# Routing lists of a four-layer gated network on one Trainium2 core: bf16 operands with the token tile innermost, and no GpSimd share

## The reference

```python
def _L3_ffn_ref(x, router_w, w1, w2):
    HID, FFN, E, K = (256, 1024, 8, 2)
    N = B * T
    x_flat = x.reshape(N, H)
    C = max(1, int(1.25 * N / E * K))
    probs = jax.nn.softmax(x_flat @ router_w.T, axis=-1)
    top_v, top_i = jax.lax.top_k(probs, K)
    top_v = top_v / jnp.sum(top_v, axis=-1, keepdims=True)
    for k in range(K):
        ...   # a token's position among those of its expert, kept if below C
        h = gelu(einsum('ech,ehf->ecf', expert_in, w1), approximate=False)
        y = einsum('ecf,efh->ech', h, w2)
        out = out + tok * (gate * keep)[:, None]
x = x + tanh(g_ffn[3]) * _L3_ffn_ref(_layernorm(x), ...)
```

## Time and profile before

| what | value |
|---|---|
| median of 3 runs | 1907.35 us (1907.02 to 1913.06) |
| the profiled execution, its own time | 1903.68 us |
| its span, first to last instruction | 1901.9 us |
| mean granted PE clock over the span | 0.913 of full |
| busy: PE, DVE, ACT, POOL | 82%, 65%, 49%, 16% of the span |
| last feed-forward's routing, logits to `f3_idx` | from 1584.65 to about 1619.5 us of the span |

### The profile page before, as it was taken

One profiled execution on the slowest core, in us unless ns is written; L12 is line 12 of the kernel. 1 busy time (PEld: TensorE's weight loads), 2 busy tenths in 40 slices (PEclk: granted clock), 3 DMA queues, 4 the chain that ended last, 5 costly groups with the idle time before them and its releaser, 6 DMA issues.

```text
span 1901.9 us, 30702 instructions
## 1 busy us (share of the span) xinstructions
PE 1558.9 (82%) x10686; PEld 1192.3 (63%) x10686; DVE 1241.1 (65%) x2782; ACT 937.2 (49%) x2055; POOL 300.9 (16%) x367
## 2 busy tenths in 40 slices
PE   4899873994788873588887999999969984799997
PEld 3666652873555542345554677788855543799997
DVE  6666648214899998766663444536359987577775
ACT  3455540323776742245554612223249971577775
POOL 2101101431121100111110000000012111243333
PEclk8899985996899987789998999999979995899999
DMA  8455244227564511635524100000167736422222
GB/s 165 61 75 84 41 147 169 42 34 148 106 104 93 89 54 47 78 47 73 73 35 172 76 1 1 0 1 1 45 78 98 114 71 256 161 39 40 43 39 28
DMA packets 86261, 144.10 MB, mean 76 GB/s; under 512 B 14031, under 2 KB 69767, under 8 KB 82937
## 3 DMA queue, kind: packets, MB, share of 16 engines
q1 hardware_dynamic: 66121, 102.76, 24.3%
q0 software_dynamic: 20016, 39.71, 13.6%
HBM read 75.50 MB, written 27.66 MB: 54 GB/s over the span
## 4 chain that ended last, share of the span: by engine, by line
PE 53%; DVE 25%; DMA 9%; issue 6%; ACT 5%; SPq 2%; POOL 0%; ACTq 0%; POOLq 0%; DVEq 0%
PE ps L1408 13%; PE ps L1512 7%; PE ps L1524 5%; DMA Qpack<-QP 5%; PE ps L1377 4%; DVE probs L2293 3%; PE ps L1048 2%; PE ps L1289 2%; PE ps L995 2%; SPq L525 2%; PE ps L904 2%; PE ps L986 2%; PE ps L1298 2%; DVE hpart L2274 2%; DVE nmax L2206 2%
## 5 line engine op out<-in xcount | busy, mean ns | idle before, releaser
L359 POOL DMA_DIRECT2D Kpack<-KP x192 | 101.1, 534 | 949.2 <-PE ps L1408 383.4
L1647 ACT ACTIVATE pT<-ps 128x512 f32<-128x512 f32 x256 | 151.8, 606 | 192.7 <-PE ps L989 98.9
L986 PE MATMUL ps<-Qpack,Kpack 99*128 99x256 bf16 (+1 forms) x768 | 166.1, 283 | 20.7 <-ACT pT L1652 8.0
L1512 PE MATMUL ps<-xgT,XNT 128*128 128x128 f32 x1248 | 146.9, 277 | 0.0
L1512 PEld LDWEIGHTS ps<-xgT,XNT 128*128 128x128 f32 x1248 | 144.0, 193 | 0.0
L955 PE MATMUL ps<-Kpack,Qpack 97*128 97x256 bf16 x512 | 103.4, 288 | 47.9 <-DMA Qpack<-QP 18.8
L2194 DVE CUSTOM_DVE_ANT_0 Vb<-ps,mask_bf 128x256 bf16<-128x256 f32 x256 | 94.9, 419 | 50.0 <-PE ps L955 49.9
L1652 ACT ACTIVATE pT<-ps,nmax 128x256 f32<-128x256 f32 x256 | 120.6, 532 | 11.9 <-DVE nmax L2206 11.4
L1408 PE MATMUL ps<-partB,h 128*128 128x512 f32 x512 | 121.1, 396 | 1.4 <-ACT xn L1904 1.4
L1408 PE MATMUL ps<-partA,h 128*128 128x512 f32 x512 | 120.4, 396 | 0.0
L2190 DVE TENSOR_REDUCE mx<-ps 128x2 f32<-128x512 f32 x128 | 84.6, 685 | 52.7 <-PE ps L955 51.9
(11 more groups left out here) (323 smaller groups left out, 3622.7 us busy)
## 6 DMA issues: line engine op xcount, KB each, us to landing
Kpack<-KP POOLq DMA_DIRECT2D x192, 128.0 KB, 5.2
Qpack<-QP SPq DMA_DIRECT2D x192, 128.0 KB, 6.9
w<-in_w SPq DMA_DIRECT2D x16, 1024.0 KB, 6.1
ctxT<-in_ctxT SPq DMA_DIRECT2D x32, 256.0 KB, 8.2
h_rows<-in_h SPq DMA_DIRECT2D x16, 512.0 KB, 7.8
h<-h_rows SPq DMA_DIRECT2D x2, 4096.0 KB, 22.1
wd<-in_wd SPq DMA_DIRECT2D x4, 1536.0 KB, 14.8
xn_rows<-xn SPq DMA_DIRECT2D x16, 256.0 KB, 2.5
```

Source lines behind the costliest of these rows:

```text
L359: eng.dma_start(Kpack[j][DH * k:DH * (k + 1)].rearrange("d (e f) t -> d e (f t)", f=HALF), KP[par][:, part]).then_inc(done, 16)
L986: mm = pe.matmul(A[h % ring][:, t], Kpack[par][0:rows, h, t * P:(t + 1) * P], Qpack[par][0:rows, h], start=True, stop=L != 0)
L1512: mm = pe.matmul(bank[:, f % 4 * P:(f % 4 + 1) * P], w1_tile[k % 2][:, c, f * P:(f + 1) * P], xgT3[k % 2][:, c], start=c == 0, stop=c == K ...
L1647: act.activation(pT[h % 8][:], A[h % 2][:], ACT.Exp).then_inc(s["exp_done"], 1)
```

## The change

`lists3` becomes `[P, PAIRS3, 6, TILES3, NT]` and `hot3` `[P, PAIRS3, P, NT]`: the token tile's number is the innermost dimension, 16 bf16 elements next to one another. `place3` and `tile3` become bf16. A table `cols3` of 128x16 bf16 (each column number sixteen times in a row) and `col_t3` (0 to 15 in bf16) are written by ACT after the softmax's exponential into the free half of `XNT`. All of DVE's operands of these operations are then bf16 with a last step of one element, the broadcast one being an outer dimension. GpSimd's two operations go to DVE, and `f3_place` and `f3_gates` go away. PE's two operands of the 32 matmuls now have 16 elements (32 bytes) from one column to the next.

```diff
-        place3 = sb("place3", [P, PAIRS3, NT], F32, f3c)
-        tile3 = sb("tile3", [P, PAIRS3, NT], F32, f3c)
+        place3 = sb("place3", [P, PAIRS3, NT], BF16, f3c)
+        tile3 = sb("tile3", [P, PAIRS3, NT], BF16, f3c)
...
-        hot3 = sb("hot3", [P, PAIRS3, NT, P], BF16, l3c)
-        lists3 = sb("lists3", [P, PAIRS3, NT, 6, TILES3], BF16, l3c)
+        hot3 = sb("hot3", [P, PAIRS3, P, NT], BF16, l3c)
+        lists3 = sb("lists3", [P, PAIRS3, 6, TILES3, NT], BF16, l3c)
...
+        cols3 = XNT[:, 1, 0:P * NT // 2].bitcast(BF16).rearrange("p (c t) -> p c t", t=NT)
+        col_t3 = XNT[:, 1, P * NT // 2:(P + 1) * NT // 2].bitcast(BF16)
...
             def ffn3(n):                       # gpsimd
-                wide = [P, PAIRS3, NT, TILES3]
-                pool.wait_ge(s["f3_place"], 1)
-                for v in range(1, 3):
-                    e = pool.tensor_tensor(lists3[:, :, :, 3 + v], lists3[:, :, :, 0], part3[v][:].unsqueeze(3).to_broadcast(wide), ALU.mult)
-                e.then_inc(s["f3_gates"], 1)
                 rows_sent(n)
...
-                pe.wait_ge(s["f3_gates"], 1)
                 for j in range(PAIRS3):
                     pe.wait_ge(s["hot"], listed + j + 1)
                     for t in range(NT):
-                        mm = pe.matmul(ps[3][:].rearrange("p a b -> p (a b)")[:, 0:6 * TILES3], hot3[:, j, t],
-                                       lists3[:, j, t].rearrange("p v i -> p (v i)"),
+                        mm = pe.matmul(ps[3][:].rearrange("p a b -> p (a b)")[:, 0:6 * TILES3], hot3[:, j, :, t],
+                                       lists3[:, j, :, :, t].rearrange("p v i -> p (v i)"),
...
                 route_exp(3)                   # scalar
+                act.activation(cols3, col[:].unsqueeze(2).to_broadcast([P, P, NT]), ACT.Copy)
+                act.activation(col_t3, col[:, 0:NT], ACT.Copy).then_inc(s["f3_cols"], 1)
...
-                per = lists3[:, :, :, 0]       # vector
-                wide = [P, PAIRS3, NT, TILES3]
-                chain(dve.tensor_tensor(per, tile3[:].unsqueeze(3).to_broadcast(wide),
-                                        col[:, 0:TILES3].unsqueeze(1).unsqueeze(1).to_broadcast(wide), ALU.is_equal))
-                dve.sem_inc(s["f3_place"], 1)
-                dve.tensor_tensor(lists3[:, :, :, 1], per, col[:, 0:NT].unsqueeze(1).unsqueeze(3).to_broadcast(wide), ALU.mult)
-                dve.tensor_scalar(lists3[:, :, :, 2], per, row[:], None, ALU.mult)
-                dve.tensor_tensor(lists3[:, :, :, 3], per, part3[0][:].unsqueeze(3).to_broadcast(wide), ALU.mult)
+                per = lists3[:, :, 0]
+                wide = [P, PAIRS3, TILES3, NT]
+                dve.wait_ge(s["f3_cols"], 1)
+                chain(dve.tensor_tensor(per, tile3[:].unsqueeze(2).to_broadcast(wide),
+                                        cols3[:, 0:TILES3].unsqueeze(1).to_broadcast(wide), ALU.is_equal))
+                dve.tensor_tensor(lists3[:, :, 1], per, col_t3.unsqueeze(1).unsqueeze(1).to_broadcast(wide), ALU.mult)
+                dve.tensor_scalar(lists3[:, :, 2], per, row[:], None, ALU.mult)
+                for v in range(3):
+                    dve.tensor_tensor(lists3[:, :, 3 + v], per, part3[v][:].unsqueeze(2).to_broadcast(wide), ALU.mult)
                 for j in range(PAIRS3):
-                    dve.tensor_tensor(hot3[:, j], place3[:, j].unsqueeze(2).to_broadcast([P, NT, P]),
-                                      col[:].unsqueeze(1).to_broadcast([P, NT, P]), ALU.is_equal).then_inc(s["hot"], 1)
+                    dve.tensor_tensor(hot3[:, j], place3[:, j].unsqueeze(1).to_broadcast([P, P, NT]), cols3, ALU.is_equal).then_inc(s["hot"], 1)
```

More of the change, by code:

```diff
@@ L331, in program @@
                  "f2_w f2_h1 f2_h2 f2_w3 f2_low f2_low_ps f2_wide f2_xstep f2_xpart f2_step f2_part f2_up f2_sil f2_hA f2_mm f2_act f2_yps f2_y f2_acc "
-                 "f3_place f3_gates f3_loaded f3_idx "
+                 "f3_cols f3_loaded f3_idx "
                  "gather0 gather1 gather2 gather3 f3_xt f3_xgT f3_up f3_w1_act f3_w1_dve f3_mid f3_ml f3_w2h f3_w2l f3_piece f3_yg f3_scatter").split()
```

## The result

| what | before | changed |
|---|---|---|
| median | 1908.28 us (22 runs) | 1914.74 us (22 runs) |
| ratio | | 1.0033, 95% interval 1.002 to 1.0046 |
| the profiled execution's own time | 1903.68 us | 1916.25 us |
| its span | 1901.9 us | 1914.5 us |

The time forecast was 1901.9 us in a range of 1900.0 to 1909.3; the change made the kernel slower. Now and then an execution of a kernel takes 2600 us or more, and every ratio in this document and its interval compare the others alone, so a ratio is not exactly the quotient of the two medians beside it.

What follows compares the result with a forecast made beforehand. The whole routing was taken to lie on the path, with DVE's 11.44 us bounding the edited stretch; cutting that to 5.95, PE's matmuls unchanged, saved 5.5 us: 1907.35 - 5.5 = 1901.9 us, range 1900.0 to 1909.3.

Steps and rivals of the forecast that it cites:

- The DVE terms: Slot table to first one-hot table in the routing: 11.44 us falls to 5.95 with paired bf16 operations, saving 5.5 us.
- the tensor_scalar: DVE's list operation on a tensor and a scalar: 0.75 us queued, bounds 0.42 (four elements a cycle) and 1.42.
- the gap behind the slot table: DVE's wait on its own semaphore between slot table and list operations: 0.147 us, kept in the new sum.
- GpSimd's cost to DVE: GpSimd working beside DVE's list operations lengthens L2837 by about 2.2 us and L2838 by at least 1.1.
- ACT's copies and the way to the first gather: ACT's two table copies end 12 us early and cost nothing; `f3_idx` to the first gather stays 0.8 us.
- moves as a block: Everything behind the routing, gathers and expert loop, starts 5.5 us earlier and is otherwise unchanged.
- the last stretch: The PE-bound loop over expert tiles, 236 us from 1652 us on, was to stay as before.
- PE's 32 matmuls: The lists' matmuls with columns 32 bytes apart: 6.31 us as before, upper bound 13.6; the lower was taken.
- a weak witness: DVE's reduction of f32 elements 32 bytes apart, 1.77 ns an element, used only for the matmuls' upper bound.
- Rival B: PE's strided reads eat the gain: its list matmuls take 9 to 13.6 us, total up to 1909.1; chance 0.25.
- Rival C: PE's weight loads slow down too and no longer overlap: 20.9 us for the 32 matmuls, total 1916.4; chance 0.08.
- Rival D: DVE pairs nothing because of the broadcast operand: gain only 0.4 us, total 1906.9; chance 0.07.

Runs made afterwards that it cites:

- gp_out: The kernel before with GpSimd's two list operations given to DVE and nothing else changed; ratio 0.9998 (0.9979 to 1.0017).
- g16_warm: The changed kernel with 110 matmuls that compute nothing used put on PE before the lists, to raise its clock; 1911.61 us in a single run.
- hot16: g2 with 16 token tiles innermost in the stationary operand `hot3` only, the moving `lists3` keeping 2; 1905.29 us in a single run.
- g2: The changed kernel with 2 token tiles innermost in both tables instead of 16, 4 bytes between PE's columns; 1906.73 us, ratio 0.9979 against before.

## Why the prediction was wrong

- *The DVE terms* were right, and a little too dear. L2833 was forecast at 0.826 us and took 0.83, the queued list operations 0.75 (1611.06 to 1611.81), the first one-hot table 1.226, and 1.28 us lie between its start and PE's. The saving was forecast at 5.5 us and was 6.04. Of that half us 0.3 is the tensor_scalar: I took 0.75 queued, it costs 0.46 (1611.81 to 1612.27), close to the 0.42 of the lower bound. Another 0.1 is the gap behind the slot table, forecast at 0.147 us and now 0.03, and 0.1 PE's start behind the first one-hot table. Here the Trainium skill's rule of four elements in a cycle ("VectorE: DVE Perf Modes", section "The perf-mode tier table") was right against my nearest row, which was a conversion from f32; this trace agrees (0.55 us for 1280 elements, against 0.82 for the paired operations).
- *GpSimd's cost to DVE* was forecast at 2.2 and at least 1.1 us; it is 2.17 and 2.06 (gp_out), the second higher because that operation is a four-a-cycle one.
- *ACT's copies and the way to the first gather:* right. 1.89 and 0.20 us, over 12.6 us early; the last softmax to the slot table takes 15.79 us as before; the lists' end to the loop's first matmul is unchanged at 6.8 us.
- *What comes after "moves as a block"*, and the last stretch "as before": not so. The wait for the fifth tile's gather became shorter, and the down matmuls became slower, -2.3 and +2.5 us that I had at nothing and that nearly cancel.
- *PE's 32 matmuls: the step that failed.* I had both ends, 6.31 and 13.6 us, and took the lower one because the half clock "leaves it twice the time for a column". What the runs showed in its place: a moving operand with 16 bytes or more between columns is read at 1.83 ns a column, at half clock and at full clock alike (g16_warm), and 1.83 is more than twice the 0.82 that PE asks for at half clock. The row that I called a weak witness, DVE's strided reduction at 1.77 ns an element, had the size within 4%; that both engines pay for the same reason isn't shown. Rival B was what happened; its end at 13.6 us was 0.7 too low. (Its lower end was wrong by its own terms: a phase of 9 us gives 1904.5 us, and not the 1902.9 that stands there.)
- *Rival C* (loads too): wrong, though its time, 1916.4 us, lies nearest to the 1914.74 measured; that is luck. The stationary operand's distance costs nothing (hot16), and PE's phase was 14.3 us and not 20.9. *Rival D*: wrong, DVE pairs with a broadcast operand, down to rows of 2 elements (g2).
- *What no term had:* the clock. Strided matmuls keep it at 0.50, so the loop starts lower for longer, 0.67 us.
- *The range* ended at 1909.3, where B's own price ended: it left nothing for B with the clock's part, nor for a median that lay 0.9 us higher in 22 runs than in 3. The changed kernel's 1914.74 is 5.4 us beyond. Of the 6.5 us between the two medians the profiles account for 2.8; for the other 3.6 no row has been found.

## What to carry to other kernels

A layout is paid for by every engine that touches it. Before a dimension is moved innermost for DVE's sake, look at what PE streams: keep four of its moving columns within 16 bytes. Two were nearly free at half clock (7.08 us for 5.90) and cost twice the time at full clock. A pair of bf16 elements innermost is all that DVE wants; that gives it the whole gain, and PE reads as fast as before. Where an uncertain price lies between two rows, the row of another engine that reads the same way said more here than an argument about clocks.

## What the runs showed of the hardware that I had not expected

- The strided stream has a price that doubles from 8 to 16 bytes and is flat from there: 5.90, 7.08, 13.94 and 14.27 us for 32 matmuls of 240 columns at 4, 8, 16 and 32 bytes. From 8 bytes on it doesn't follow PE's clock. It holds for the moving operand alone.
- PE may be busy all the time and still lose its clock: while it was streaming a strided operand the granted clock went from 1.00 to 0.50 within two us (g16_warm), and stayed there to the end of the lists. With 4 bytes between columns it rose while PE streamed (g2: 0.50 for the first 5.0 of the 5.90 us, 1.00 for the rest).
- Fillers on PE can pay where a clock would fall: with 155 of them, which compute nothing, the way from the first matmul of the lists to the end of the loop's first 64 was 3.6 us shorter than in g2.
- Matmuls that the edit leaves alone became slower: the down matmuls on `mh3` had a mean of 288 ns in g2 for 284 before, 2.5 us over 35 tiles, and the cause is open.
- GpSimd's operations beside DVE cost it more than the work that they took over: 5.86 us of POOL work made two DVE operations 4.2 us longer, and DVE does that work itself in 2.8.
